# Four fused layers on one core: turned probabilities copied by ACT, the softplus's add moved to ACT, and a new order of pieces

## The reference, cut to what matters

```
# layer 0: Mamba, then two mixtures of experts
delta = softplus(dt @ W_dt.T + b_dt)              # (L, 256)
dA, dBx = exp(delta[..., None] * A), delta[..., None] * Bm * xc[..., None]
h = dA_t * h + dBx_t ; y_t = h . C_t              # scan over L, 16 states for each of 256 channels
# layer 1: RWKV's wkv scan, a ternary linear layer. layer 2: window attention, routed linear layer
# layer 3: attention with Q, K, V rotated by 2x2 blocks, then a shared and 8 routed experts
p = softmax(2 * (q @ k.T) / scale + 2 * bias ...) ; o = p @ V      # 1024 x 1024 for each batch
h = gelu(x @ w1.T + b1) ; out = h @ w2.T + b2     # 9 experts of width 512, all run for all tokens
```

## Time and profile before

| | us |
|---|---|
| median of 3 runs | 1496.78 |
| lowest and highest run | 1489.78, 1500.4 |
| the profiled execution's own time | 1495.27 |
| its span, first to last instruction | 1493.5 |

### The profile page before, as it was taken

How to read it: one execution, slowest core, us unless ns; L and a number is a source line. 1 busy time by engine, 2 the same in 40 slices (tenths; PEclk the granted TensorE clock), 3 DMA queues, 4 the chain that set the end, 5 groups by cost and what they waited for, 6 DMA issues and landing times.

```text
span 1493.5 us, 13005 instructions
## 1 busy us (share of the span) xinstructions
PE 1156.2 (77%) x3838; PEld 559.6 (37%) x3850; DVE 930.5 (62%) x2126; ACT 713.4 (48%) x1358; POOL 587.0 (39%) x404
## 2 busy tenths in 40 slices
...
DMA packets 11270, 17.76 MB, mean 12 GB/s; under 512 B 1304, under 2 KB 7584, under 8 KB 10688
## 3 DMA queue, kind: packets, MB, share of 16 engines
...
## 4 chain that ended last, share of the span: by engine, by line
PE 36%; DVE 9%; ACT 5%; issue 2%; POOL 1%; POOLq 0%; DVEq 0%; ACTq 0%
PE bankE L1749 8%; PE bankE L1827 5%; PE bankE L1247 3%; PE bankS L1791 2%; PE bankS L1776 2%; PE bankE L1309 2%; PE bankE L1268 1%; ACT b_pr L1145 1%; PE bankS L1729 1%; DVE c_tw L1919 1%; PE bankE L622 1%; PE bankE L1297 1%; PE bankE L581 1%; PE bankE L1296 1%; DVE b_xr L1424 1%
## 5 line engine op out<-in xcount | busy, mean ns | idle before, releaser
L752 DVE TENSOR_TENSOR_SCAN hs<-dA,carry,bankS 128x512 f32<-128x512 f32 x128 | 156.7, 1266 | 3.3 <-DVE bankS L744 0.5
L1722 ACT ACTIVATE c_h<-bankE,C 128x512 f32<-128x512 f32 x144 | 99.0, 687 | 124.3 <-PE bankE L1827 123.9
L1749 PE MATMUL bankE<-c_h,c_w 128*128 128x512 f32 x288 | 150.7, 605 | 8.9 <-DVE c_tw L1919 6.8
L330 POOL TENSOR_TENSOR hc<-hs,cb 128x1024 f32<-128x1024 f32 x56 | 131.7, 2352 | 53.3 <-DVE hs L752 50.2
L307 POOL TENSOR_TENSOR cv<-cv,hc 128x1024 f32<-128x1024 f32 x56 | 132.5, 2366 | 4.4
L1618 POOL TENSOR_TENSOR c_acc<-c_acc,c_tw 128x512 f32<-128x512 f32 x32 | 40.8, 1274 | 198.0 <-DVE c_tw L1919 197.9
L1919 DVE SCALAR_TENSOR_TENSOR c_tw<-bankE,C,wb_ready 128x512 f32<-128x512 f32 x32 | 24.0, 751 | 128.0 <-PE bankE L1749 128.0
L1827 PE MATMUL bankE<-c_fH,c_w1H 128*128 128x512 f32 x144 | 101.1, 702 | 0.0
L445 ACT ACTIVATE sg<-bankE,C 128x512 f32<-128x512 f32 x80 | 54.5, 686 | 88.4 <-PE bankE L581 88.1
L744 DVE TENSOR_TENSOR bankS<-dx,bankS 128x1024 f32<-128x1024 f32 x64 | 78.4, 1225 | 8.4 <-PE bankS L510 7.7
L395 ACT ACTIVATE dA<-dl,Aneg 128x512 f32<-128x512 f32 x128 | 80.8, 709 | 3.3 <-DVE dl L735 3.2
...
## 6 DMA issues: line engine op xcount, KB each, us to landing
...
```

The lines of the kernel that those rows point to most:

```text
L330: pool.tensor_tensor(dst[:, :, :], hs[:, k % HS, :, :], cb[:, k % 2, :].unsqueeze(1).to_broadcast([P, HV, G]), ALU.mult).then_inc(s["hc_re ...
L752: V.tensor_tensor_scan(hs[:, k % HS, h, :], dA[:, (HV * k + q) % DA, :], dbx[:, h, :], carry[:, k, h:h + 1], ALU.mult, ALU.add).then_inc(s ...
L1722: act.activation(h[:, n % 3, :], E[k % 2][:, :], ACT.Gelu_apprx_tanh, bias=col("b1_3", k)).then_inc(s["fs_ready"], 1)
L1749: pe.matmul(E[2][:, :], w2[:, k, :], h[:, n % 3, :], start=(f == 0), stop=(f == FB3 - 1)).then_inc(s["fdown"], 1)
```

## The change

It does three things.

1. `keep_turned` leaves DVE. The 32 copies of turned probabilities are issued by ACT in the same pieces `cT` and `ct`, with the same semaphores.
2. In the softplus, u = 1+e is no longer computed by DVE (`tensor_scalar`, in `aF4`). ACT computes it by an Identity with a bias of one, after both logs (in `aF8`), and signals a new semaphore `sp_one`. DVE's first operation of `aF9` waits for it.
3. `ORDER` is another permutation of the same 1020 pieces.

```
@@ scalar, piece F8 @@
                     act.activation(spa[:, h, :], spe[:, h, :], ACT.Ln, bias=one[:, 0:1]).then_inc(s["sp_ln"], 1)
+                for h in range(HV):
+                    act.activation(spu[:, h, :], spe[:, h, :], ACT.Identity, bias=one[:, 0:1]).then_inc(s["sp_one"], 1)
@@ vector, pieces F4 and F9 @@
-                for h in range(HV):
-                    at_least(V, s["exp_done"], i, HV, h + 1)
-                    inc(V.tensor_scalar(spu[:, h, :], spe[:, h, :], 1.0, None, ALU.add))
             elif p == "F9":
                 wait()
                 for h in range(HV):
+                    at_least(V, s["sp_one"], i, HV, h + 1)
                     inc(V.scalar_tensor_tensor(spu[:, h, :], spu[:, h, :], -1.0, spe[:, h, :], ALU.add, ALU.subtract))
@@ last layers, scalar @@
+            elif p[0] == "T" or p[0] == "t":
+                t, c = NT * i + k, int(p[0] == "t")
+                act.wait_ge(s["c_pTp"], 2 * t + c + 1)
+                act.activation(pT[:, 4 * c:4 * c + 4, (t % 4) * P:(t % 4 + 1) * P],
+                               S[2][:, :].rearrange("p (n q) -> p n q", q=P), ACT.Copy).then_inc(s["c_pT"], 1)
@@ last layers, vector @@
-            elif p[0] == "T" or p[0] == "t":
-                keep_turned(NT * i + k, int(p[0] == "t"))
```

More of the change, by code:

```diff
@@ L96 @@
 ORDER = [(p[0], p[1:].split(".")[0], int(p.split(".")[1])) for p in """
[L97 to L144, removed]
+    aF1.0 aF5.0 aF6.0 aF2.0 aF0.0 aF7.0 aF3.0 aF8.0 aF4.0 aF9.0 aA0.0 aN0.0 an0.0 ao0.0 aN1.0 an1.0 ao1.0 aN2.0 aA1.0 an2.0 ao2.0 aN3.0
```

51 lines of the change are left out of this document (47 added, 4 removed).

## The result

| | us |
|---|---|
| changed kernel, median of 7 runs (1506.59 to 1508.74) | 1508.06 |
| kernel before, median of 7 runs (1488.3 to 1500.4) | 1489.78 |
| ratio, with its 95% interval | 1.0093 (1.0065 to 1.0120) |
| profiled execution of the changed kernel: time, span | 1508.35, 1506.6 |

The changed kernel is 0.9% slower, 14 us by the ratio and 13.1 by the two profiled executions (1508.35 - 1495.27). The two medians are 18.3 us apart, as four of the seven runs of before lie at 1488 to 1490 us and three at 1497 to 1500. The runs of before scatter over 12 us here and over 21 in a later set, those of the changed kernel over 2. In three later sets of runs, on chips 4, 9 and 11, the medians of before were 1497.51, 1496.08 and 1498.97 us; the changed kernel was timed in this set alone, so its loss is known only to lie between 9 and 18 us.

What follows compares the result with a forecast made beforehand. Bound by the scan stream in group 0, two streams waiting in turn in groups 2 and 3, a norm chain at the window layer's end, then PE. 1495.3 + 8.3 + 1.5 - 2 - 1.5 - 5 = 1496.6, forecast 1497 us, range 1472 to 1519.

Steps and rivals of the forecast that it cites:

- within 1%: Whole kernel: the forecast with its neighbours, 1481 to 1511 us, no change that a measurement could tell; chance 0.50.
- The softplus: Mamba's groups 0 to 3: adds behind both logs delay the corrected log; 2.5 + 1.2 + 2.6 + 2.0 = 8.3 us later.
- the third rival: Groups 1 to 3 absorb the softplus's delay: 2.5 in place of 8.3, loads nothing, 1489 us; shares the forecast's 0.50.
- Table loads: ACT: 64 loads besides the start's, 60 before; six more in Mamba 1.5 us later, two fewer in last experts 1.5 earlier.
- The order of Mamba's pieces: Mamba: a saved Exp load in group 1 gives 1.3 us; six extra loads in groups 2 and 3 cost 1.5.
- The copies: 32 copies of turned probabilities, DVE to ACT: gain 0 to 4.9 us, loss 0 to 8; taken as 2 us earlier.
- The 3.5 us that copies and loads were to gain in the last stretch: Last attention and experts: 2 us earlier from copies on ACT, 1.5 us earlier from two table loads saved.
- The second rival: 1232 to 1330 us: ACT becomes the bound where attention tiles lie among expert chunks; 9.6 us for copies, 1521 us; chance 0.23.
- ACT's 61 of 75 us: 1232 to 1307 us: with about 12 copies, ACT's busy time goes from 53.7 to some 61 us, under PE's 71.6.
- the wait for Gelus: Last experts: PE lost 7.9 us in 9 places to late Gelus before; forecast to stay under 12 us.
- The end of the window layer: After 1135 us: two score tiles and a pair of turns fill PE's 8.3 us gap; 5 us earlier, bounds 0 and 17.6.
- all other moves: Other order moves, by a few pieces, and POOL splits cS1 to cS8: costed at nothing; uncovered, under 2 us.

Runs made afterwards that it cites:

- e1: Both code edits (softplus add and copies on ACT) in the order of before, against the kernel before: 1528.26 us, ratio 1.0198.
- e2: The new order with the code of before, against the kernel before: 1519.20 us, ratio 1.0138.
- e9: The changed kernel with the softplus's add back on VectorE, copies on ACT and new order kept: 1500.67 us, ratio to before 1.0029.
- e7: The kernel before with only the copies moved to ACT, in the order of before: 1514.77 us, ratio 1.0110.
- e5: The kernel before, its code kept, with the new order only up to the end of Mamba and its experts (first 511 pieces): 1493.10 us, ratio 0.9971.
- e11: The changed kernel with the nine POOL splits of the window layer at old places and the softplus's add on VectorE: 1494.74 us, ratio to before 0.9998.
- e12: The changed kernel with nine POOL splits and ten pieces (bV2.0 to bO2.0) in old order, softplus's add on VectorE: 1486.93 us, ratio to before 0.9957.
- e8: The changed kernel with only the nine POOL splits (cS0.0 to cS8.0) back at old places in the window layer: 1496.62 us, ratio to before 0.9999.
- e13: The changed kernel with only the splits cS6.0 and cS7.0 moved, some 60 pieces later: 1499.58 us, ratio to before 1.0025.
- e10: The changed kernel with nine POOL splits and ten more pieces (bV2.0 to bO2.0) in the order of before: 1492.43 us, ratio to before 0.9974.

## Why the prediction was right, and where it was not

The range held the time, and the chance of 0.50 was on "within 1%". That is partly luck. The sum was 12 us short, the ratio's interval (0.65 to 1.20%) reaches over the mark of 1%, and the terms were worse than the sum shows: errors of opposite sign cancelled, and either half of the change alone lies beyond the range's upper end of 1519 us (e1 1528.26, e2 1519.20).

- **The softplus** was right in place and nearly in size. Timeline of the changed kernel, group 0, against the earlier trace rows:

```profile
32.00 1.33 ACT L382 ACTIVATE dA<-dA,one 128x512 f32<-128x512 f32 x2
33.23 1.32 ACT L384 ACTIVATE dA<-dA,one 128x512 f32<-128x512 f32 x2
...
34.05 1.29 DVE L728 SCALAR_TENSOR_TENSOR dA<-dA 128x512 f32<-128x512 f32 x2 [4.96 <-ACT dA L384]
35.26 1.28 DVE L732 TENSOR_TENSOR dA<-dA 128x512 f32<-128x512 f32 x2
...
37.89 0.58 PE L502 MATMUL bankS<-bc,sel 96*128 96x512 bf16 x1 [11.58 <-DVE dl L735]
```

  The corrected log starts at 35.26 (35.25 forecast), and PE waits 11.58 us (11.6). Four groups cost 7.0 us at 792 (changed against e2) and 7.4 timed (e9), where the sum had 8.3, or 9.6 without the load that the order saves. From the start of the first log to the corrected log (L382 to L732) it is 3.27 us in each group, against 0.75, 0.75, 1.34 and 1.21 before: 2.5, 2.5, 1.9 and 2.1 more, as forecast to 0.1 us. But e2, the new order with the code of before, already has 0.75, 2.33, 2.62 and 2.59: in groups 1 to 3 the pieces that the new order puts between `aF4` and `aF9` keep DVE busy, and it starts L728 with no idle time. So against e2 the first scans of the four groups pay 2.4, 2.3, 1.0 and 0.8. In the old order the same edit costs more: e1 stands 17 us behind e7 at 792, of which these local delays are 9; where the rest comes from was not followed. That it is absorbed, the third rival, is wrong.
- **Table loads:** 65, as counted, each of 1283 ns. The order of Mamba's pieces was mis-sized: the sum had -1.3 and +1.5; the runs have -6.6 at 792 (e2) and 4 us at the end (e5). The two agree when the late trace of before is allowed for: the three traces of the old order stand at -2.5 in the mean, the five of the new order without the softplus edit (e2, e5, e9, e11, e12) at -6.7. That gain hid the softplus in the table's first columns.
- **The copies** take ACT 0.597 us, as the earlier trace rows, and in the new order PE waits little for them:

```profile
L1701 ACT ACTIVATE c_pT<-bankS x32: 575/597/629, 1082.4 to 1358.7; 128x512 f32<-128x512 f32 x32
...
  PE bankS L1734: 5.3, 6
```

  The 3.5 us that copies and loads were to gain in the last stretch are 0 (13.2 to 13.4). The sum treated the copies apart from the order, and that was its largest error of method: they cost 16 us in the old order (e7) and save 18.5 in the new one by the medians, 16 by the ratios (e2 1519.20, e9 1500.67). The second rival, ACT as the bound among the tiles, has its size in the old order (8.4 us between first and last Gelu in e7, 9.6 priced), but the trace does not show its mechanism: from 1178 to 1300 ACT is busy 74.2 of 122 us in e7, PE waits 5.4 us in 5 places for the copies from 1176 on, and the clock of the window is 0.96 where before has 1.00. The new order avoids these waits. Of the signs, ACT's 61 of 75 us were 56.4, as 8 copies fell into that window and not 12; the wait for Gelus (PEld, 7.9 us before) was 11.1, under the 12.
- **The end of the window layer** was to give 5 us. The tiles do stand in the gap:

```profile
1147.74 1.88 PE L1781 MATMUL bankS<-c_kT,c_qT 128*128 128x512 f32 x4
1149.46 0.60 PE L1734 MATMUL bankS<-ident,c_L 128*128 128x128 f32 x4
1151.32 0.63 PE L1734 MATMUL bankS<-ident,c_L 128*128 128x128 f32 x4 [1.26 <-ACT c_pT L1701]
1151.78 1.88 PE L1781 MATMUL bankS<-c_kT,c_qT 128*128 128x512 f32 x4
1156.25 0.66 PE L1174 MATMUL bankE<-ident,b_pT 128*128 128x128 f32 x4 [2.58 <-DVE b_pT L1353]
```

  That is 5.0 us of work in a gap of 8.35 (8.3 before). But the gap of before was not empty, which the prediction passed over. It held two turns, 1.75 us:

```profile
1136.84 0.66 PE L1729 MATMUL bankS<-ident,c_L 128*128 128x128 f32 x4 [1.49 <-ACT c_L L1697]
1142.14 1.09 PE L1729 MATMUL bankS<-ident,c_L 128*128 128x128 f32 x4 [4.64 <-DVE c_pT L1905]
```

  So 3.2 us are new in the gap. The shift falls from 14.6 at 1053 to 12.6 where the gap starts (L1302, 1134.19 and 1146.74), is the same behind it, and 13.6 at the last sum: 1 us in the end. Where the rest went was not followed.
- **The step that failed** is the sentence on all other moves, above all the POOL splits: "I cost them at nothing, under cover of POOL's idle time; uncovered, they delay a product by one split, under 2 us." POOL was idle enough, and none of the three places starts with a late product of POOL. But the splits slow the norms that DVE does beside them, PE waits for those, and half clock follows. e8 prices this at 9 to 14 us and e13 at 6.5 to 10 for two splits of nine. The ten pieces around `bK7.2` are 4 us more (e10). Added up, 7.0 softplus - 6.6 Mamba's order + 9.3 splits + 4 ten pieces - 1 window end = 12.7, against 13.1. This is no proof that nothing is missing: the terms mix traces and times, each is sure to 3 or 4 us only, and the 16 us of the copies show that such terms need not add up.

The Trainium skill, page "SBUF — State Buffer", section "Who interferes with whom", says that VectorE and GpSimd share one pair of SBUF ports, that a tensor_scalar within SBUF can need it, and that it is locked for a whole instruction. The traces agree, and not for the splits alone. A norm of L1933 takes 338 ns at the median. The one of 1423 ns, from 1037.77 beside the split's subtraction, ends 0.08 us after it (1039.19 and 1039.11); the longest, 1932 ns from 1042.75, ends 0.08 us after a product of POOL's window layer (L1052). The kernel before already has norms of L1353 of 1932 and 1424 ns with a median of 342 to 344, so the sign was there to be read. By that rule the splits' places would have been a rival of their own.

What stays open: why e11 gains less over e8 than e12 over e10 (the intervals are 0.2% wide on either side), why the copies lose in one order what they save in the other, and, as POOL's other products slow norms too, what share of the two kernels' time that is.
